# Causal attention by head on one core: q and k by one projection, their copies laid out by DMA, and a new order of calls

## The chip, the cores and the metric

The kernel runs on one core of a Trainium2 chip. The metric is the device time of one execution in microseconds (us); lower is better. TensorE is PE in the profile, VectorE is DVE, ScalarE is ACT, GpSimd is POOL, and SyncE, which only issues DMAs here, is SP. PE's weight loads are listed apart, as PEld.

## What is computed

The program is an attention layer with a small graph network, three layer norms with residuals, and then two layers of local attention with a feed-forward block. The change touches only the first part. Per batch (2) and head (16), with 1024 tokens and heads of 64 features, the reference computes:

```python
xn = layer_norm(x, gamma_in)
q = (xn @ Wq).reshape(b, n, HEADS, DHEAD).transpose(0, 2, 1, 3) * scale      # scale = 1/8
k = (xn @ Wk).reshape(b, n, HEADS, DHEAD).transpose(0, 2, 1, 3)
v = (xn @ Wv).reshape(b, n, HEADS, DHEAD).transpose(0, 2, 1, 3)
sim = jnp.where(causal_mask, mask_value, jnp.einsum('bhid,bhjd->bhij', q, k))
attn = jax.nn.softmax(sim, axis=-1)
out = jnp.einsum('bhij,bhjd->bhid', attn, v)
adj = jnp.clip(attn + eye, 0.0, 1.0)          # by head
for l in range(2):
    h = adj @ (feats @ gnn_w[l] + gnn_b[l]) / deg
    feats = gelu(h + feats)
out = out + feats @ lin_w + lin_b
return layer_norm(out @ Wo, gamma_out)
```

## The kernel before

**Heads.** The 32 pairs of batch and head are numbered t = 0 to 31 (NH = 32). Each engine runs a program of its own, written out by hand as a list of calls; its instructions run in that order, and semaphores (`p_...` raised by PE, `a_...` by ACT, `d_...` by DVE, `w_...` by POOL) say when an operand is ready. One pass of the loop over t is called a head below. It holds the scores and the product with the values of head t, the row maxima (`smax`) of head t + 1, the projection (`proj`) of head t + 2, the second graph layer (`graph2`, `graph2b`) of head t - 1 and of head t, and the output product (`tailT`, `tail`) of head t - 2.

**Two parts for each number.** Matmuls read operands rounded to fp32r, so every operand is kept as a rounded part (hi) and a remainder (lo). A product of two such numbers is the sum of hi·hi, hi·lo and lo·hi.

**q and k.** `WD` holds the weights of a head twice side by side, so that the projection on PE (L520 to L538) gives the same 64 features in partitions 0 to 63 and 64 to 127 of a bank. There are four of them for each head: k and q, and two column halves c of 512 tokens; each is three matmuls. ACT (`proj`, L1024 to L1032) writes the hi part of all 128 partitions into `K1` or `Q1`. DVE (`lower`) writes the lo part: that of q (L1509) over partitions 64 to 127 of `Q1`, that of k (L1507) into partitions 0 to 63 of `K2`. POOL (`upper`, L1340) copies the hi part of q into `Q2`. A tile of scores (L618, L619) is then K1·Q1, which is k_hi·(q_hi + q_lo), plus K2·Q2, which is k_lo·q_hi; `K2` has two rows of ones under it and `Q2` the negated row maximum as hi and lo, so that the maximum comes off in the same matmul.

**The row maximum.** `smax` on PE (L581) makes score tiles with queries in the partitions, DVE takes their maxima (L1532), and after the last of 12 tiles combines them and splits them in hi and lo in `NM` (L1537, L1539, L1541). `mrow` turns them into rows: eight matmuls with an identity (L598, four for each half c), then two copies of 2x512 on ACT (L1051) into `Q2`.

**Tiles.** The causal triangle of 1024x1024 is cut into 12 tiles of 128 keys by 512, 384, 256 or 128 queries. For each tile there are two matmuls of scores, ACT's two exponentials (L1061 and L1062, into `Es` and `Eh`), DVE's remainder `El` (L1554), three matmuls of `av` (L636 to L638) and two of `graph2` (L671, L672). Score tiles alternate between banks 2 and 3, so that `scores(t, k)` waits for the exponential of tile k - 2; `smax` tiles alternate between banks 0 and 1. `graph2` ends each half with four matmuls (L676) into bank 5, which ACT copies out (`hopend`, L1095) before `graph2(t, 4)` may write there.

**DMA.** Between the loads at the start and the end of the first part, SP issues nothing at all. The second part of the program copies values between partitions by DMA (L453 and L455: 64 partitions x 2 KB, 128 KB each).

## Time and profile before

| | us |
|---|---|
| median of 3 runs (1625.11 to 1625.67) | 1625.44 |
| the profiled execution | 1620.1 |
| its span on the core, first to last instruction | 1618.3 |
| from the start to the first tile of scores | 39.3 |
| heads 1 to 29, from 81.64 to 1056.46 | 974.8 |
| the second part, from about 1131 to the end | about 487 |

The granted clock was 0.972 on average. Of the span PE was busy for 1469.1 us (91%), DVE for 1285.7 (79%), ACT for 1054.1 (65%), POOL for 419.2 (26%). In the rows, "x12" is a count, and the time after "busy" or before the engine's name is that of the group. In a timeline a row is start, duration, engine, line, operation, output<-input and shape; matmuls overlap, so the start of one to the start of the next tells how far it moves PE on, not its duration.

### The profile page before, as it was taken

Reading aid. Unit: us, or ns where it says so; the run is one execution under the profiler, and the core shown is the slowest. Engines: PE = TensorE matmul, PEld = TensorE weight load, DVE = VectorE, ACT = ScalarE, POOL = GpSimd, SP = SyncE. Lnnn points to the kernel's source line nnn. Section 1 sums busy time; section 2 is a strip of 40 time slices with the busy share of each in tenths; the row PEclk is TensorE's granted clock in tenths of the full one; section 3 lists DMA queues with packets and bytes.
Section 4 is the critical chain, followed back from the end, with each engine's and each line's share of the span. In section 5 each row is a group of like instructions: output and inputs, shape, how many; then the busy total and the mean of one; then the engine's idle time right before and its main releaser. Section 6 shows DMA issues by size and latency. Waiting matters only on the chain.

```text
span 1618.3 us, 30002 instructions
## 1 busy us (share of the span) xinstructions
PE 1469.1 (91%) x10578; PEld 1157.4 (72%) x10578; DVE 1285.7 (79%) x3374; ACT 1054.1 (65%) x2403; POOL 419.2 (26%) x544
## 2 busy tenths in 40 slices
PE   5999999999999999999999999998467899999996
PEld 4678877788788887788877888777245566666664
DVE  6588887888888788888888888875577888878875
ACT  3577676666676767767667676764245777787673
POOL 2122223222332222322233222211322342223221
PEclk9899999999999999999999999999778999999999
DMA  4000000000000000000000000000400010000100
GB/s 122 1 1 2 1 1 1 1 1 1 1 1 1 1 1 1 1 1 1 1 1 1 2 1 1 1 1 1 111 14 20 17 26 19 21 21 17 28 18 20
DMA packets 23199, 19.67 MB, mean 12 GB/s; under 512 B 8414, under 2 KB 18314, under 8 KB 23050
## 3 DMA queue, kind: packets, MB, share of 16 engines
q1 hardware_dynamic: 23050, 17.76, 4.3%
q8 instruction: 84, 1.38, 0.4%
q14 instruction: 65, 0.53, 0.1%
HBM read 8.84 MB, written 1.05 MB: 6 GB/s over the span
## 4 chain that ended last, share of the span: by engine, by line
issue 33%; PE 27%; DVE 20%; ACT 10%; POOL 8%; DMA 0%; SPq 0%; POOLq 0%; DVEq 0%; ACTq 0%
ACT t L1213 5%; PE PS L671 3%; DVE t L1554 2%; PE PS L672 2%; PE PS L706 2%; POOL t L1307 2%; DVE t L1585 2%; POOL t L1350 2%; PE PS L618 2%; PE PS L581 2%; POOL t L1340 2%; PE PS L619 1%; DVE t L1756 1%; DVE t L1782 1%; DVE t L1740 1%
## 5 line engine op out<-in xcount | busy, mean ns | idle before, releaser
L1061 ACT ACTIVATE t<-PS 128x512 f32<-128x512 f32 (+3 forms) x384 | 191.3, 498 | 222.3 <-PE PS L621 136.5
L1554 DVE TENSOR_TENSOR t<-t 128x512 fp32r<-128x512 f32 (+3 forms) x384 | 246.6, 642 | 48.8 <-ACT t L1062 47.3
L1532 DVE TENSOR_REDUCE t<-PS 128x1 f32<-128x512 f32 (+3 forms) x384 | 208.0, 549 | 24.2 <-PE PS L581 24.0
L1062 ACT ACTIVATE t<-PS 128x512 fp32r<-128x512 f32 (+3 forms) x384 | 191.7, 499 | 0.0
L1350 POOL TENSOR_TENSOR t<-t 128x256 f32<-128x256 f32 x64 | 39.2, 613 | 551.7 <-DVE t L1574 551.7
L671 PE MATMUL PS<-t 128*128 128x512 f32 (+3 forms) x384 | 141.8, 369 | 21.6 <-ACT t L1095 21.6
L1213 ACT ACTIVATE t<-PS,t 128x128 f32<-128x128 f32 x256 | 113.2, 464 | 67.4 <-DVE t L1786 67.3
L1415 POOL TENSOR_TENSOR t<-t 128x16 f32<-128x16 f32 x32 | 92.8, 2900 | 239.7 <-DVE t L1742 239.7
L636 PE MATMUL PS<-t 128*66 128x512 f32 (+3 forms) x384 | 137.3, 358 | 16.2 <-DVE t L1554 16.2
L581 PE MATMUL PS<-t 128*128 128x512 f32 (+3 forms) x384 | 141.0, 378 | 3.6 <-DVE t L1532 2.7
L618 PE MATMUL PS<-t 128*128 128x512 f32 (+3 forms) x384 | 143.6, 374 | 0.1
L619 PE MATMUL PS<-t 66*128 66x512 f32 (+3 forms) x384 | 134.5, 350 | 0.0
L638 PE MATMUL PS<-t 128*66 128x512 f32 (+3 forms) x384 | 129.6, 338 | 0.0
L637 PE MATMUL PS<-t 128*66 128x512 f32 (+3 forms) x384 | 129.1, 336 | 0.0
L672 PE MATMUL PS<-t 128*128 128x512 f32 (+3 forms) x384 | 129.0, 348 | 0.0
L1307 POOL TENSOR_TENSOR t<-t 128x2 f32<-128x2 f32 (+1 forms) x42 | 33.8, 804 | 272.4 <-DVE t L1462 180.7
L671 PEld LDWEIGHTS PS<-t 128*128 128x128 f32 x384 | 73.4, 191 | 37.4 <-ACT t L1095 26.1
L1551 DVE SCALAR_TENSOR_TENSOR t<-t 128x128 f32<-128x128 f32 x256 | 72.6, 284 | 29.0 <-ACT t L1061 29.0
L618 PEld LDWEIGHTS PS<-t 128*128 128x128 f32 x384 | 74.4, 194 | 17.0 <-issue 2.5
L581 PEld LDWEIGHTS PS<-t 128*128 128x128 f32 x384 | 75.1, 196 | 13.0 <-DVE t L1532 4.7
L1032 ACT ACTIVATE t<-PS 128x512 fp32r<-128x512 f32 x128 | 76.3, 596 | 12.1 <-PE PS L538 8.3
L672 PEld LDWEIGHTS PS<-t 128*128 128x128 f32 x384 | 73.7, 192 | 9.8
(191 smaller groups left out, 4152.6 us busy)
## 6 DMA issues: line engine op xcount, KB each, us to landing
t<-t SPq DMA_DIRECT2D x60, 128.0 KB, 2.3
t<-in_L_ffn_wqkv SPq DMA_DIRECT2D x2, 768.0 KB, 6.9
t<-in_L_attn_Wv SPq DMA_DIRECT2D x2, 512.0 KB, 7.9
t<-in_c_rot SPq DMA_DIRECT2D x2, 512.0 KB, 4.7
out<-t SPq DMA_DIRECT2D x4, 256.0 KB, 2.3
t<-in_L_ffn_w SPq DMA_DIRECT2D x2, 341.0 KB
t<-in_L_attn_x SPq DMA_DIRECT2D x2, 256.0 KB, 3.2
t<-in_L_attn_Wq SPq DMA_DIRECT2D x1, 512.0 KB, 5.5
```

What stands on the lines that cost most here:

```text
L581: m = e.matmul(bank(b)[:, 0:hi - lo], Q1[r][:, ib * P:(ib + 1) * P], K1[r][:, lo:hi], start=True, stop=not diag)
L618: e.matmul(b[:, 0:n], K1[r][:, jb * P:(jb + 1) * P], Q1[r][:, i0:i0 + n], start=True, stop=False)
L619: m = e.matmul(b[:, 0:n], K2[r][:, jb * P:(jb + 1) * P], Q2[r][:, i0:i0 + n], start=False, stop=not diag)
L636: e.matmul(dst, VH[r][:, jb, :], Eh[:, o:o + n], start=(jb == 0), stop=False)
L638: m = e.matmul(dst, VH[r][:, jb, :], El[:, o:o + n], start=False, stop=(jb == 4 * c + 3))
L671: e.matmul(dst, F2[:, jb, :], Eh[:, o:o + n], start=(jb == 0), stop=False)
L672: e.matmul(dst, F2[:, jb, :], El[:, o:o + n], start=False, stop=False).then_inc(p_hop.up((t, k)), 1)
L1061: e.activation(Es[:, k % NS, 0:n], b[:, 0:n], ACT.Exp).then_inc(a_es.up((t, k)), 1)
L1062: e.activation(Eh[:, o:o + n], b[:, 0:n], ACT.Exp).then_inc(a_eh.up((t, k)), 1)
L1213: m = e.activation(E[u][:, n, :], bank(SB + j)[:, c * P:(c + 1) * P], ACT.Exp, bias=nmx[u][:, n:n + 1], scale=sc8[w][:, n:n + 1], accum_ou ...
L1532: e.tensor_reduce(n[:, c, ib:ib + 1], bank(k % 2)[:, 0:hi - lo], AX.X, ALU.max, negate=True).then_inc(d_max.up((t, k)), 1)
L1554: e.tensor_tensor(El[:, o:o + n], Es[:, k % NS, 0:n], f32(Eh[:, o:o + n]), ALU.subtract).then_inc(d_el.up((t, k)), 1)
```

## The change

All of it is in the first part of the program. The two heads' weights Wk and Wq stand side by side in `WD`, which is half as large, and one projection gives k in partitions 0 to 63 and q in 64 to 127. ACT writes both hi parts into `K1`, with a scale by partition from the new tile `qsc` (1 and 0.125), and DVE both lo parts into `Q1`. SP then moves what the scores need elsewhere: `part` copies q_hi to `Q2` and k_lo to `K2` (four transfers of 64 partitions x 2 KB), `double` copies k_hi to the other half of `K1` and q_hi back into `Q1` (two of 64 x 4 KB). `smax` and `scores` wait for `double`. POOL's `upper` is gone, and `widen` does half as much.

The maximum is no longer split: one matmul in full f32 turns the eight columns into eight rows, ACT copies 8x128 into the new tile `MR`, and SP's `mrow` moves it (4 KB) into one row of `Q2`. `K2` and `Q2` have 65 rows.

The order of calls changes on all engines. The projection of head t + 2 on PE stays near the end of head t; `smax(t + 1, 0)`, which opened the head, now stands behind the third tile of scores.

```diff
+            def part(t):
+                r = t % RB
+                for c in range(2):
+                    sl = slice(c * 512, (c + 1) * 512)
+                    q.wait_ge(*a_hi[t, c])
+                    e.dma_start(f32(Q2[r][0:64, sl]), f32(K1[r][64:128, sl])).then_inc(s_apart[c], 16)
+                    q.wait_ge(*d_low[t, c])
+                    e.dma_start(f32(K2[r][0:64, sl]), f32(Q1[r][0:64, sl])).then_inc(s_apart[c], 16)
+            def double(t):
+                r = t % RB
+                q.wait_ge(*apart(t, 0))
+                q.wait_ge(*apart(t, 1))
+                e.dma_start(f32(K1[r][64:128, :]), f32(K1[r][0:64, :])).then_inc(s_twice, 16)
+                e.dma_start(f32(Q1[r][0:64, :]), f32(Q2[r][0:64, :])).then_inc(s_twice, 16)
+            def mrow(t):
+                q.wait_ge(*a_row[t])
+                e.dma_start(f32(Q2[t % RB][64:65, :]).rearrange("a (k p) -> a k p", k=8), f32(MR[:])).then_inc(s_row, 16)
+            part(0)
+            double(0)
+            for t in range(NH):
+                if t + 1 < NH:
+                    part(t + 1)
+                mrow(t)
+                if t + 1 < NH:
+                    double(t + 1)
...
-                e.matmul(bank(b), WD[t % RB][:, 0, i, :], xh[:, x0_:x1_], start=True, stop=False)
-                e.matmul(bank(b), WD[t % RB][:, 1, i, :], xh[:, x0_:x1_], start=False, stop=False)
-                e.matmul(bank(b), WD[t % RB][:, 0, i, :], xl[:, x0_:x1_], start=False,
-                         stop=True).then_inc(p_proj.up((t, which, c)), 1)
+                e.matmul(bank(b), W[:, 0, :], xh[:, x0_:x1_], start=True, stop=False)
+                e.matmul(bank(b), W[:, 1, :], xh[:, x0_:x1_], start=False, stop=False)
+                e.matmul(bank(b), W[:, 0, :], xl[:, x0_:x1_], start=False, stop=True).then_inc(p_proj.up((t, c)), 1)
...
-                q.wait_ge(*d_low[t, "q", 1])
-                q.wait_ge(*a_hi[t, "k", 1])
+                q.wait_ge(*twice(t))
...
-                for k in range(4):
-                    m = e.matmul(bank(4)[0:66, k * P:(k + 1) * P], NM[:, 4 * c + k, :], identR[:], start=True, stop=True)
+                e.matmul(bank(4)[0:8, 0:P], nm[t % 2][:, 0, :], identF[:], start=True, stop=True).then_inc(p_row.up(t), 1)
...
-                q.wait_ge(*a_row[t, 1])
-                q.wait_ge(*w_q2[t, 1])
-                q.wait_ge(*d_low[t, "q", 1])
-                q.wait_ge(*d_low[t, "k", 1])
+                q.wait_ge(*row_ready(t))
+                q.wait_ge(*twice(t))
...
-                e.activation(T1[:, c * 512:(c + 1) * 512], bank(b), ACT.Copy, scale=sc).then_inc(a_hi.up((t, which, c)), 1)
+                e.activation(K1[t % RB][:, c * 512:(c + 1) * 512], bank(b), ACT.Copy, scale=qsc[:, 0:1]).then_inc(a_hi.up((t, c)), 1)
...
-                if which == "k":
-                    m = e.tensor_tensor(K2[r][0:64, sl], bank(b)[0:64, :], f32(K1[r][0:64, sl]), ALU.subtract)
-                else:
-                    m = e.scalar_tensor_tensor(Q1[r][64:128, sl], bank(b)[64:128, :], 0.125, f32(Q1[r][64:128, sl]),
-                                               ALU.mult, ALU.subtract)
+                e.scalar_tensor_tensor(Q1[r][:, sl], bank(b), qsc[:, 0:1], f32(K1[r][:, sl]), ALU.mult,
+                                       ALU.subtract).then_inc(d_low.up((t, c)), 1)
...
-                smax(t + 1, 0)
                 scores(t, 0)
...
+                scores(t, 2)
+                smax(t + 1, 0)
```

On PE, at the end of a head, the rows of before are these: L536 to L538 are a projection, L598 is `mrow`, L657 `graph1`, L671 and L672 `graph2`, L618 the next head's first scores behind L581, its first `smax`.

```order
L536 MATMUL PS<-t 128x512
L537 MATMUL PS<-t 128x512
L538 MATMUL PS<-t 128x512
L598 MATMUL PS<-t 66x128 x4
L657 MATMUL PS<-t 128x130 x4
L536 MATMUL PS<-t 128x512
L537 MATMUL PS<-t 128x512
L538 MATMUL PS<-t 128x512
L671 MATMUL PS<-t 128x512
L672 MATMUL PS<-t 128x512
L671 MATMUL PS<-t 128x256
L672 MATMUL PS<-t 128x256
```

The changed kernel has there, with `graph2` at L694, L695 and L699, `graph1` at L680, `mrow` at L624 and the scores of the next head at L641:

```order
L694 MATMUL PS<-t 128x512
L695 MATMUL PS<-t 128x512
L680 MATMUL PS<-t 128x130 x4
L694 MATMUL PS<-t 128x256
L695 MATMUL PS<-t 128x256
L624 MATMUL PS<-t 8x128
L694 MATMUL PS<-t 128x384
L695 MATMUL PS<-t 128x384
L694 MATMUL PS<-t 128x128
L695 MATMUL PS<-t 128x128
L699 MATMUL PS<-t 128x128 x4
L694 MATMUL PS<-t 128x512
```

No projection is left in the last stretch, and `mrow` is a single matmul, behind which five tiles of `graph2` still stand before the scores that need its result.

On DVE, at the same place, before has two remainders of q (L1509) and two of k (L1507), and three small operations for the maximum behind the last two reductions (L1532):

```order
L1532 TENSOR_REDUCE t<-PS 128x1 x2
L1537 TENSOR_TENSOR t<-t 128x4
L1539 CAST t<-t 128x8
L1541 TENSOR_TENSOR t<-t 128x8
L1600 TENSOR_TENSOR t<-t 128x4x64
L1509 SCALAR_TENSOR_TENSOR t<-PS,t 64x512 x2
L1608 TENSOR_TENSOR t<-t 128x4x64
L1507 TENSOR_TENSOR t<-PS,t 64x512
```

The changed kernel has the remainders (L1498) first, and the reductions (L1520) behind them:

```order
L1583 TENSOR_TENSOR t<-t 128x4x64
L1498 SCALAR_TENSOR_TENSOR t<-PS,t 128x512 x2
L1520 TENSOR_REDUCE t<-PS 128x1
L1591 TENSOR_TENSOR t<-t 128x4x64
L1520 TENSOR_REDUCE t<-PS 128x1
L1524 TENSOR_TENSOR t<-t 128x4
```

Two remainders instead of four stand there, one small operation instead of three, and the maximum is ready only after the remainders.

SP has nothing in this stretch before. The changed kernel has seven transfers for each head, `part` (L435, L437), `mrow` (L448) and `double` (L443, L444):

```order
L435 DMA t<-t 64x512
L437 DMA t<-t 64x512
L435 DMA t<-t 64x512
L437 DMA t<-t 64x512
L448 DMA t<-t 1x8x128
L443 DMA t<-t 64x1024
L444 DMA t<-t 64x1024
```

`double` of head t + 2 is issued behind `mrow` of head t + 1, and so not before that maximum is out of ACT.

## Rows read from the trace of the kernel before

**Rows 1.** Windows: length, busy us (count) PE, PEld, DVE, ACT, POOL, clock, DMA.
```profile
451.85:485.27 33.42, 32.36 (x221) 26.98 (x220) 27.42 (x74) 23.19 (x50) 8.69 (x15) 1.00 0.01 1
81.64:1056.46 974.82, 937.46 (x6365) 781.12 (x6364) 819.22 (x2267) 673.52 (x1422) 261.23 (x418) 1.00 0.00 1
```
**Rows 2.** Waits of PE from 81.64 to 1056.46: total us, times, longest us.
```profile
PE PS L671 <- ACT t L1095: 19.6, 29, 0.7
PE PS L636 <- DVE t L1554: 14.2, 29, 0.8
```
**Rows 3.** Timeline of PE in head 12: start us, duration us.
```profile
456.74 1.95 PE L706 MATMUL PS<-t 128*128 128x128 f32 x16
458.44 0.47 PE L618 MATMUL PS<-t 128*128 128x512 f32 x1
...
474.89 0.40 PE L536 MATMUL PS<-t 128*128 128x512 f32 x1
...
475.59 0.39 PE L636 MATMUL PS<-t 128*66 128x512 f32 x1
...
478.86 0.40 PE L598 MATMUL PS<-t 128*66 128x128 f32 x4
479.10 1.11 PE L657 MATMUL PS<-t 66*128 66x130 f32 x8
```
**Rows 4.** Groups of DVE by line: busy us, mean ns, idle before.
```profile
L1507 DVE TENSOR_TENSOR t<-PS,t 64x512 fp32r<-64x512 f32 x64 | 43.3, 677 | 1.0
L1509 DVE SCALAR_TENSOR_TENSOR t<-PS,t 64x512 fp32r<-64x512 f32 x64 | 41.9, 692 | 7.5 <-ACT t L1032 6.5
...
L1480 DVE SCALAR_TENSOR_TENSOR t<-PS,t 128x512 fp32r<-128x512 f32 x4 | 3.0, 748 | 1.2 <-ACT t L1010 1.2
```
**Rows 5.** Groups of ACT by line.
```profile
L1032 ACT ACTIVATE t<-PS 128x512 fp32r<-128x512 f32 x128 | 76.3, 596 | 12.1 <-PE PS L538 8.3
...
L1051 ACT CAST t<-PS 2x512 fp32r<-2x512 f32 x64 | 37.0, 578 | 13.6 <-PE PS L598 12.8
...
L1010 ACT ACTIVATE t<-PS,t 128x512 fp32r<-128x512 f32 x4 | 2.8, 689 | 0.9 <-PE PS L484 0.9
```
**Rows 6.** DMA issues of the page: count, KB each, median us to landing.
```profile
t<-t SPq DMA_DIRECT2D x60, 128.0 KB, 2.3
```
**Rows 7.** The same transfers' line: time of one issue in ns, min/median/max.
```profile
L455 SPq DMA_DIRECT2D t<-t x28: 461/590/1210, 1157.9 to 1552.3; - x28
```
**Rows 8.** A window of the second part (last: DMA share, GB/s).
```profile
1300.00:1360.00 60.00, 56.37 (x509) 38.62 (x509) 50.25 (x100) 45.11 (x124) 20.15 (x10) 1.00 0.09 21
```
**Rows 9.** Timeline of ACT at the end of head 12.
```profile
482.90 0.58 ACT L1095 COPY t<-PS 128x512 f32<-128x512 f32 x1 [0.44 <-PE PS L676]
```
**Rows 10.** Timeline of ACT at the start of head 12.
```profile
452.60 0.60 ACT L1061 ACTIVATE t<-PS 128x512 f32<-128x512 f32 x1 [0.44 <-PE PS L621]
453.09 0.59 ACT L1062 ACTIVATE t<-PS 128x512 fp32r<-128x512 f32 x1
```
**Rows 11.** Timeline of PE in head 30: waits before two groups.
```profile
1081.80 0.28 PE L636 MATMUL PS<-t 128*66 128x128 f32 x1 [1.05 <-DVE t L1554]
...
1082.96 0.45 PE L598 MATMUL PS<-t 128*66 128x128 f32 x4 [0.76 <-DVE t L1541]
```
**Rows 12.** A window of head 30 (columns as in Rows 1).
```profile
1085.00:1086.00 1.00, 1.00 (x8) 0.98 (x7) 0.68 (x2) 0.00 (x0) 0.25 (x1) 0.50 0.00 0
```
**Rows 13.** Timeline of DVE in head 12: a difference of two SBUF tiles.
```profile
475.74 1.39 DVE L1554 TENSOR_TENSOR t<-t 128x128 fp32r<-128x128 f32 x1
```
**Rows 14.** Timeline of POOL at the same time.
```profile
475.69 1.28 POOL L1371 TENSOR_TENSOR t<-t 128x512 f32<-128x512 f32 x1 [1.75 <-DVE t L1615]
```
**Rows 15.** Timeline of PE: the first tiles of smax.
```profile
22.74 0.62 PE L581 MATMUL PS<-t 128*128 128x512 f32 x2 [0.81 <-DVE t L1509]
```
**Rows 16.** Windows at the start (columns as in Rows 1).
```profile
24.00:28.00 4.00, 3.88 (x27) 3.12 (x27) 2.65 (x7) 1.29 (x4) 0.00 (x0) 1.00 0.27 83
...
36.00:40.00 4.00, 2.71 (x11) 1.77 (x11) 1.06 (x4) 1.15 (x2) 0.00 (x0) 0.54 0.00 0
```

More of the change, by code:

```diff
@@ L352, in program @@
         s_vs = [sem(f"vs{i}") for i in range(4)]
+        s_apart = [sem(f"s_apart{c}") for c in range(2)]
+        s_twice = sem("s_twice")
+        s_row = sem("s_row")
         ld = {n: sem("l_" + n) for n in ("xa", "xb", "xc", "id", "wq", "wk", "gin", "wv", "w0", "wv2", "cm", "wg", "ww1",
@@ L729, in tensor @@
                     turn(t - 4, 6)
+                graph2(t - 1, 9)
                 scores(t, 1)
+                graph2(t - 1, 6)
+                scores(t, 2)
+                smax(t + 1, 0)
                 smax(t + 1, 1)
+                scores(t, 3)
                 tailT(t - 2, 0)
@@ L738, in tensor @@
                     linear(1, 6)
-                tailT(t - 2, 1)
-                graph2(t - 1, 6)
-                scores(t, 2)
-                scores(t, 3)
+                scores(t, 4)
+                tail(t - 2, 0)
                 smax(t + 1, 3)
@@ L1045, in projv, with mrow @@
                 e.copy(VH[r][:, ks, 0:DH], pv[:, :, 0:DH]).then_inc(a_v.up((t, c)), 1)
[L1047 removed]
+            def mrow(t):
                 if t >= NH:
                     return
[L1050 to L1051 removed]
+                q.wait_ge(*p_row[t])
+                if t:
+                    q.wait_ge(*row_ready(t - 1))
+                e.copy(MR[:], bank(4)[0:8, 0:P]).then_inc(a_row.up(t), 1)
             def scores(t, k):
@@ L1685, in vector @@
                     began(1)
+                smax(t + 1, 0)
                 scores(t, 1)
@@ L1698, in vector @@
                 smax(t + 1, 4)
-                scores(t, 5)
+                share(t - 1, 1)
                 smax(t + 1, 5)
```

282 lines of the change are left out of this document (113 added, 169 removed).

## The prediction

> **What bounds the kernel now.** I read the busy time by windows first. A steady head takes 33.42 us and PE is busy for 32.36 of them; DVE with 27.42 and ACT with 23.19 have room [rows 1]. Over heads 1 to 29 it is 937.46 of 974.82 us. The waits of PE come next: only two kinds matter, 19.6 us before the tile of graph2 that needs bank 5 emptied by ACT, and 14.2 us before the small tile of av that needs DVE's remainder, 0.7 and 0.5 us for each head [rows 2]. So the first part is bound by PE almost throughout, and work taken from PE should come off the time, unless the operands now come too late. The second part (some 487 us) is not touched.
>
> **PE, removed.** In the timeline one projection starts at 474.89 and the next group at 475.59, so three matmuls move PE on by 0.70 us [rows 3]. Two of four projections go: 1.40 us. Since a group costs up to 0.05 more where the weights ahead of it aren't hidden, I take 1.45. The eight small matmuls of mrow move PE on by 0.24 us for each four (478.86 to 479.10), 0.48 in all. The one f32 matmul that replaces them isn't in this trace with 8 output rows; the nearest row is the f32 product of 128x128, 16 matmuls (two for each product) in 458.44 - 456.74 = 1.70 us, so 0.21 us [rows 3]. Its bounds are 0.06, if it were as cheap as one of the old, and 0.21; I take the latter, as the same type and length. Net: 1.45 + 0.48 - 0.21 = **1.7 us for each head**.
>
> **The other engines.** DVE loses four remainders of 0.68 us and gains two of about 0.75, the row with a scale by partition [rows 4]: 2.74 - 1.50 = 1.24 us, and two small operations more. ACT loses four copies of 0.60 and two of 0.58, and gains two of 0.69 and one small one, bounded by 0.58 [rows 5]: at least 1.6 us less. POOL loses two copies. None of these engines sets the pace at 31 to 32 us a head (27.42 - 1.24 is 26.2), so this gain is priced at nothing; what it buys is slack for the waits below.
>
> **The waits PE has.** The gap of 0.68 us before graph2(t, 4) remains: the last product into bank 5 must be copied by ACT, a copy of 0.58 us behind 0.44 us of idle time [rows 9], and nothing in the new order stands between the two on PE. The gap before av(t, 11) should go, because a projection less and graph2b stand ahead, and DVE has more time: -0.5 us. New ones may come. At the head's start, the third scores tile (which needs the exponential of the first) stands after only two tiles of scores and two of graph2, some 1.5 us of columns; ACT starts 0.75 us after PE's start at 451.85 and has both exponentials out at 453.68, 1.83 us [rows 1, 10]. That is a wait of about 0.3 us. And DVE, whose order waits for smax tile 6 before it does the remainder of scores tile 5, is late for smax tile 11 by 0 to 0.45 us if I follow its list with the durations of the trace; I take 0.2. Sum: old gaps down by 0.5, new ones up by 0.5. **No change.**
>
> **The row of the maximum.** Behind mrow on PE stand five tiles of graph2: 8 matmuls of 512 or 384 columns, two of 128 and four small ones, 2.3 us at 0.23 for each 512 columns, plus the gap. With mrow's own 0.2 and, counted from start to start, 0.85 for the gap, the next scores start 3.5 us after mrow. The chain it must hide: matmul 0.2, its result 0.2 later, ACT's copy 0.3 (up to 0.58, [rows 5]), and the transfer. The nearest row is 128 KB in 2.3 us from issue to landing [rows 6]; 4 KB can hardly take longer. Sum 3.0 to 3.3 us. It fits by 0.2 to 0.5 us, as long as ACT is free, which it is: gelu2 ahead of it must wait for POOL, which by my count is done some 2 us before mrow's result. I price it at nothing. If the cover is gone, each 0.1 us costs 3 us in all.
>
> **part and double.** One issue takes SP 0.46 to 0.59 us [rows 7]. The projection of head t + 2 ends 3.9 us before mrow; ACT and DVE need 0.69 and 0.75 for the last half [rows 4, 5]. Both remainders are ready some 2 us after the last projection, and the last of the four small transfers lands 2.3 us later, at about the time of mrow's copy on ACT. double is issued behind mrow's transfer, 1.3 us after mrow began on PE. Its length isn't in the trace. The transfers of the second part move 21 GB/s at a share of 0.09 [rows 8], 233 GB/s when all 16 engines work, so 128 KB take 0.56 us and 256 KB 1.12. One such transfer would land after 2.3 + 0.56 = 2.9 us and the second, queued behind it, 1.1 us later: 4.0 us, so 5.3 us after mrow. PE wants it at smax(t + 2, 0), behind the 3.5 us above and 1.9 us of scores and graph2: 5.4 us. Bounds: 2.3 us (as if bytes cost nothing) is far inside, and half the rate would be 6.2 us, a wait of 2.1 us for each head. I take the row's rate and a price of nothing, but this is the thinnest cover in the change.
>
> **A rule about these transfers.** In rows, 128 KB take 2.3 us [rows 6]. The Trainium skill, "DMA: Bandwidth & Descriptors", section "Anatomy of one DMA", gives about 2.0 us for any transfer plus its bytes at 436 GB/s. By that page double would be an estimate of 2.0 + 1.2 = 3.2 us for both; no row here shows that rate.
>
> **POOL against DVE.** A difference of two SBUF tiles on DVE that should take 0.28 us took 1.39 beside an operation of POOL of 1.28 [rows 13, 14]. In the new order POOL's long addition for graph2b comes behind feats(t, 0) and meets DVE's feats(t, 0): DVE is held up by some 0.4 us there, ahead of the remainders. The maximum still comes before PE asks for it. Priced at nothing.
>
> **Start and end.** The first smax tile was at 22.74 [rows 15]. Now it needs remainders, four small transfers and double. The queues are busy with loads until about 26 us (share 0.27 between 24 and 28, [rows 16]), so double lands at 29 to 31, 6 to 8 us later. But the second projection and both of v are then done, and what follows is bound by twelve maxima on DVE instead of those and the remainders of head 1, four of 0.68 us [rows 4]. Then 2.5 us for the row's transfer. Net 2 us later, -2 to +6. The clock was at 0.54 from 36 to 40 already [rows 16]. Head 30 has no projection: it gains 0.2.
>
> **The sum.** 29 steady heads x 1.7 = 49 us, head 0 about 2, the start costs 2: 49 us. On the profile's own 1620.1 that is 1571; the median is 5 us above that execution, so **1576 us**.
>
> **Rivals.** (a) *The cover of a transfer is too thin.* Landing times here are a median of a part of the program where few are in flight; here seven follow each other. A wait of 0.5 to 1.5 us for each head on smax(t + 2, 0) or on scores(t + 1, 0) gives 15 to 45 us back: 1591 to 1621. For it: my margins are 0.1 and 0.2 to 0.5 us. Against: the sums take the longer of the values. (b) *The order on DVE becomes the wait.* Every smax tile waits for the maximum two before. If DVE's idle wait for tile 6 pushes the rest back by 0.5 us more than I counted, it is 1590. Against: 26.2 us of work in 31.7. (c) *Slower than before.* If double takes 6 us or more, PE waits 2 us or more in each head. In head 30 PE waited 1.05 and 0.76 us shortly after one another, and then had a granted clock of 0.50, the 1.2 GHz level, for over 3 us [rows 11, 12], which costs half of that time. The threshold is thus near 1.8 us: beyond it each head loses the wait and 1.7 us more, 3.5 in place of the 1.7 won, and the kernel takes 1625 + 29 x 1.8 = 1678. The Trainium skill has this as a rule: "TensorE: Matmul & The Clock Gate", section "HAM oscillation", tells of a kernel that waits for a DMA in every step and starts every step at the low clock. By that rule, the trace of head 30 agrees; the 29 steady gaps of 0.7 us are followed by no such fall. (d) *More than the matmuls.* ACT and DVE run less late, and the remaining gap shrinks too: up to 0.5 us for each head, 1562.
>
> **Chances.** Forecast with its own bounds, 1562 to 1590: 0.62. (a) 0.20. (b) 0.06. (c) 0.05. (d) 0.07. The range leaves out the upper half of (a), (c), and the outer part of (d): 1563 to 1606. About 0.2% (3 us) is what a measurement of this kernel can tell from no change. Only (c) is slower; a wait that eats exactly the gain is the only way to no change: faster 0.93, same 0.02, slower 0.05.
>
> **What would show it.** PE busy in a steady head at 30.6 to 30.7 us and the head at 31.5 to 32.0. Waits of PE: L694 (graph2) on ACT 0.7; small ones on the third scores tile and on smax; none on a DMA at scores or smax. double landing 3 to 4 us after its issue. What makes it wrong: DMA as a releaser of PE with over 0.3 us a head, or a granted clock under 1.00 in the steady heads.

## The result, and the profile after

The changed kernel takes **1607.2 us** (median; 1605.8 to 1609.0), the kernel before 1625.4 beside it on the same chip: a ratio of 0.989, with a 95% interval of 0.987 to 0.991. The forecast was 1576 us with a range of 1563 to 1606. So the sign was right, the gain is 18 us instead of 49, and the time lies just outside the range. The profiled execution took 1606.2 us, and its span is 1604.5.

First the windows that answer to [rows 1]: head 12, heads 1 to 29, the start up to the first scores tile, and head 0.

```profile
core 0: us, PE busy (x) PEld busy (x) DVE busy (x) ACT busy (x) POOL busy (x), PEclk, DMA share, GB/s
451.37:483.80 32.43, 31.49 (x209) 25.46 (x209) 24.17 (x70) 21.37 (x47) 6.98 (x13) 1.00 0.16 34
...
92.10:1043.70 951.60, 913.44 (x6017) 736.81 (x6016) 727.75 (x2151) 619.66 (x1335) 216.34 (x357) 1.00 0.16 33
0.00:47.19 47.19, 21.69 (x91) 16.10 (x91) 20.67 (x65) 9.29 (x16) 8.34 (x29) 0.81 0.54 138
47.19:92.10 44.91, 42.54 (x196) 28.48 (x197) 23.29 (x70) 20.41 (x45) 3.81 (x8) 0.79 0.14 29
```

A steady head went from 33.42 to 32.43 us, and PE's busy time in it from 32.36 to 31.49, where 30.65 was forecast. DVE and ACT fell as counted. The span's balance is this, with the boundaries of before at 39.26 and 81.64 us. The first scores tile comes 7.9 us later (forecast: 2). Head 0 takes 44.9 us where it took 42.4, 2.5 more (forecast: 2 less). Heads 1 to 29 take 951.6 in place of 974.8, 23.2 less (forecast: 49). The rest is 1.0 shorter. Together that is 13.8 us of span.

The waits of PE that answer to [rows 2], in heads 1 to 30 (total us, times, longest us):

```profile
PE PS L694 <- ACT t L1111: 20.2, 30, 0.7
PE PS L613 <- DVE t L1520: 8.6, 15, 0.8
PE PS L613 <- DMA t<-t: 3.9, 7, 0.8
PE PS L680 <- ACT t L1085: 2.7, 17, 0.2
```

The wait of graph2 for ACT stayed, as forecast. The 14.2 us before av(t, 11) are gone. Three small kinds are new: smax tile 11 for DVE, the first smax tile for a transfer in seven heads (2, 5, 8, 11, 17, 20, 23), and graph1(t, 1) for ACT's copy.

The end of head 12 on PE, which answers to [rows 3] (start us, duration us):

```profile
475.21 0.48 PE L572 MATMUL PS<-t 128*128 128x512 f32 x1
475.53 0.39 PE L573 MATMUL PS<-t 128*128 128x512 f32 x1
475.76 0.40 PE L574 MATMUL PS<-t 128*128 128x512 f32 x1
...
480.08 0.39 PE L624 MATMUL PS<-t 128*8 128x128 f32 x2
480.39 0.44 PE L694 MATMUL PS<-t 128*128 128x384 f32 x1
```

Two things can be read from the start times. The f32 mrow moves PE on by 0.31 us (480.08 to 480.39), not 0.21. And two equal matmuls can differ: the first of the projection, behind the small ones of graph2b, moves PE on by 0.32 us (475.21 to 475.53), the second by 0.23 (475.53 to 475.76). The 0.09 us are a weight load that shows because what stands ahead of it is short. PE's weight loads at the same place say so:

```profile
475.19 0.19 PEld L572 LDWEIGHTS PS<-t 128*128 128x128 f32 x1
475.30 0.19 PEld L573 LDWEIGHTS PS<-t 128*128 128x128 f32 x1
475.53 0.19 PEld L574 LDWEIGHTS PS<-t 128*128 128x128 f32 x1
```

The weights of the first matmul begin to load at 475.19, 0.02 us ahead of their own matmul; those of the second begin 0.23 us ahead of theirs (475.30 and 475.53). I call such a place an **exposed load**. No view counts it as a wait: it is "busy" time of PE.

So I went through the starts of PE in one head and split each step from start to start: the columns at 2.4 GHz (0.21 us for 512; 0.11 for 128 columns of plain f32), the waits the profile records, and what is left. Where more than 0.045 us is left and no wait is recorded, it is an exposed load. These places leave 0.05 to 0.13 us each. In head 12 of the changed kernel and of the kernel before, the weight load of such a matmul begins 0.04 us ahead of it (median), and that of the other long matmuls 0.23 us. Other choices for the limits move the column by up to 0.2 us and two places. Two kernels of the next section stand in the table too: the new order alone with the old data path, and the new data path alone with the old order. All are heads at a clock of 1.00.

| one steady head, us | columns | exposed loads (places) | recorded waits | other | head |
|---|---|---|---|---|---|
| before | 29.11 | 2.14 (28) | 1.06 | 1.13 | 33.43 |
| new order alone | 29.11 | 2.81 (33) | 1.59 | 1.23 | 34.74 |
| new data path alone | 27.56 | 2.27 (27) | 3.91 | 1.40 | 35.14 |
| the change | 27.56 | 3.00 (34) | 0.94 | 0.93 | 32.43 |

The columns fell by 1.55 us. Then 0.86 us came back in the column of exposed loads, with six more places and some dearer ones, and "other" fell by 0.20. The net of 0.66 us is the larger part of what is missing in PE's busy time (31.49 and not 30.65).

"Other" holds, beside small remainders, the step into each recorded wait, which is 0.16 to 0.18 us longer than columns and wait together and counts as busy. In head 12, four matmuls of L699 start at 481.02 and the next group at 482.30: of these 1.28 us, 0.45 are columns and 0.67 the recorded wait. The kernel before has two recorded waits (of 0.1 us or more) in this head, the change three, the new order alone four, the new data path alone three.

The transfers, which answer to [rows 6]: the page, and the lines of `double` by themselves (L443, then L444). Those of `part` still land after 2.3 us (median).

```profile
t<-t SPq DMA_DIRECT2D x64, 256.0 KB, 3.4
```
```profile
L443 SPq DMA_DIRECT2D t<-t x32: 462/479/526, 29.9 to 1041.5; - x32
...
DMA to landing us min/median/max: 2.9/2.9/3.1
```
```profile
L444 SPq DMA_DIRECT2D t<-t x32: 580/597/597, 30.4 to 1042.0; - x32
...
DMA to landing us min/median/max: 3.6/3.7/4.9
```

The estimate of 2.9 us for the first transfer of `double` was met. The second, from its own issue 0.5 us later, takes 3.7, and up to 4.9 in some heads.

### The profile page after: what moved, and what is told of

It is laid out like the page before. It is cut to its first block, busy times and chain, and to the rows that moved or that the text cites. A ratio compares the mean times of both kernels' runs of the same rounds, so it can differ in the third digit from the quotient of the medians.

```text
span 1604.5 us, 29173 instructions
## 1 busy us (share of the span) xinstructions
PE 1444.8 (90%) x10194; PEld 1109.6 (69%) x10194; DVE 1187.4 (74%) x3247; ACT 995.6 (62%) x2307; POOL 370.2 (23%) x480
## 4 chain that ended last, share of the span: by engine, by line
PE 43%; DVE 25%; issue 13%; ACT 11%; DMA 3%; POOL 3%; SPq 1%; DVEq 0%; POOLq 0%; ACTq 0%
ACT t L1222 5%; DVE t L1520 4%; PE PS L613 4%; PE PS L729 3%; PE PS L708 3%; PE PS L694 3%; DVE t L1537 3%; PE PS L641 3%; DMA t<-t 3%; PE PS L642 2%; PE PS L695 2%; PE PS L661 2%; PE PS L659 2%; PE PS L660 2%; PE PS L680 2%
## 5 line engine op out<-in xcount | busy, mean ns | idle before, releaser
L1520 DVE TENSOR_REDUCE t<-PS 128x1 f32<-128x512 f32 (+3 forms) x384 | 211.3, 551 | 81.4 <-PE PS L615 56.8
L1537 DVE TENSOR_TENSOR t<-t 128x512 fp32r<-128x512 f32 (+3 forms) x384 | 212.3, 553 | 10.9 <-ACT t L1078 10.8
L694 PE MATMUL PS<-t 128*128 128x512 f32 (+3 forms) x384 | 150.2, 391 | 22.1 <-ACT t L1111 21.6
L613 PE MATMUL PS<-t 128*128 128x512 f32 (+3 forms) x384 | 141.4, 392 | 24.5 <-DMA t<-t 12.5
L641 PE MATMUL PS<-t 128*128 128x512 f32 (+3 forms) x384 | 149.8, 390 | 2.7 <-DMA t<-t 2.2
L642 PE MATMUL PS<-t 65*128 65x512 f32 (+3 forms) x384 | 134.4, 350 | 0.0
L695 PE MATMUL PS<-t 128*128 128x512 f32 (+3 forms) x384 | 129.2, 345 | 0.0
L613 PEld LDWEIGHTS PS<-t 128*128 128x128 f32 x384 | 73.4, 198 | 41.8 <-DVE t L1520 20.2
L694 PEld LDWEIGHTS PS<-t 128*128 128x128 f32 x384 | 73.3, 191 | 38.2 <-ACT t L1111 26.1
L641 PEld LDWEIGHTS PS<-t 128*128 128x128 f32 x384 | 75.0, 195 | 20.5 <-ACT t L1078 9.9
L680 PEld LDWEIGHTS PS<-t 66*128 66x128 f32 x512 | 64.6, 190 | 24.2 <-ACT t L1085 18.3
L1111 ACT COPY t<-PS 128x512 f32<-128x512 f32 x64 | 37.4, 585 | 67.6 <-PE PS L699 67.6
```

The costliest lines, as they stand in the source:

```text
L613: m = e.matmul(bank(b)[:, 0:hi - lo], Q1[r][:, ib * P:(ib + 1) * P], K1[r][:, lo:hi], start=True, stop=not diag)
L641: e.matmul(b[:, 0:n], K1[r][:, jb * P:(jb + 1) * P], Q1[r][:, i0:i0 + n], start=True, stop=False)
L642: m = e.matmul(b[:, 0:n], K2[r][:, jb * P:(jb + 1) * P], Q2[r][:, i0:i0 + n], start=False, stop=not diag)
L694: e.matmul(dst, F2[:, jb, :], Eh[:, o:o + n], start=(jb == 0), stop=False)
L695: e.matmul(dst, F2[:, jb, :], El[:, o:o + n], start=False, stop=False).then_inc(p_hop.up((t, k)), 1)
L1520: e.tensor_reduce(n[:, c, ib:ib + 1], bank(k % 2)[:, 0:hi - lo], AX.X, ALU.max, negate=True).then_inc(d_max.up((t, k)), 1)
```

## The experiments

Twelve kernels were run, in three groups, each beside the kernel before on the same chip (medians 1623.7, 1622.0 and 1622.6 us). Where this text says "less" or "later" with no other name, it compares with the changed kernel, from which all start but one (the first of the pair below) and the two that start from the combined kernel. The kernel before itself differs by up to 3.4 us between these chips, so a difference of a few us in the time alone shows little; such readings rest on the windows.

The start adds to this. In the profiled executions of four kernels whose start is the same as the changed kernel's (projection twice, graph1 later, DVE's order, no mask) head 0 took 48.9 to 50.1 us at a granted clock of 0.71 or 0.72, and not 44.9 at 0.79.

### Is PE still what sets the pace?

```diff
+                if t > 1:
+                    e.matmul(bank(b), W[:, 0, :], xh[:, x0_:x1_], start=True, stop=False)
+                    e.matmul(bank(b), W[:, 1, :], xh[:, x0_:x1_], start=False, stop=False)
+                    e.matmul(bank(b), W[:, 0, :], xl[:, x0_:x1_], start=False, stop=True)
                 e.matmul(bank(b), W[:, 0, :], xh[:, x0_:x1_], start=True, stop=False)
```

> Each of the two projections of a head from head 2 on is issued twice, so that TensorE gets six more matmuls a head and nothing else changes. If TensorE's own work sets the length of a head (31.5 us busy of 32.4), the copies cost their whole time, about 1.4 us a head, 41 us in all: about 1648 us. If waits set it, the copies fill them and the time stays between 1607 and 1620 us.

Measured: 1647.5 us (1645.5 to 1649.8), 40 us more. A steady head:

```profile
470.10:503.92 33.82, 32.88 (x216) 26.59 (x215) 23.83 (x70) 21.37 (x47) 7.07 (x13) 1.00 0.15 32
```

Six matmuls more cost 1.39 us of busy time and 1.39 us of the head. PE sets the pace, and the price of a projection, 0.7 us each, was right. What the change takes away is thus not lost to another engine.

### The order alone, and the data path alone

The first kernel is the one before with the change's order of calls on all engines; its two projections more stand together behind graph2(t, 2), directly ahead of mrow, and its second mrow behind graph2(t, 1). The end of a head in its list on PE (its lines 789 to 797):

```python
                av(t, 11)
                graph2(t, 0)
                graph1(t, 1)
                graph2(t, 2)
                proj(t + 2, "k", 0, 0)
                proj(t + 2, "k", 1, 1)
                mrow(t + 1, 0)
                graph2(t, 1)
                mrow(t + 1, 1)
```

> The kernel before with the new order of calls alone: four projections, eight matmuls for the maximum, POOL's copies and no transfers; the k projections stand behind graph1(t, 1) on PE, the start is that of before. Theory order: of the 0.7 us a head that the change wins less than forecast, 0.5 are weight loads that the new order leaves exposed (a short matmul ahead of a full weight load costs 0.1; 30 such places in a head before, 37 after) and the rest two new waits, less the one that goes. The order alone should then cost 0.2 to 0.5 us a head: 1631 to 1640. Rival: the order is as good or better by itself (it removes the wait of 0.5 before av 11) and the loss comes from the new data path: 1610 to 1625.

Measured: 1685.0 us (ratio 1.037, 1.033 to 1.040), far more than both theories had. Its head 12, and its waits from 92 to 1100 us:

```profile
480.26:515.00 34.74, 33.15 (x222) 26.86 (x221) 26.28 (x74) 23.23 (x50) 8.53 (x15) 1.00 0.00 1
```
```profile
PE PS L671 <- ACT t L1094: 18.9, 28, 0.7
PE PS L598 <- ACT t L1050: 18.0, 28, 0.7
PE PS L581 <- DVE t L1530: 8.3, 15, 0.8
PE PS L657 <- ACT t L1068: 4.6, 28, 0.2
```

PE does exactly the work of the kernel before and is busy 33.15 us instead of 32.36, 0.79 more. In the table the exposed loads grow by 0.67 us, 33 places for 28. That is the plainest evidence for the missing term: **the new order costs PE's time in each head where no wait is to be seen**. How much is less plain, since the steps into two more recorded waits account for some 0.3 of the 0.79 us; 0.4 to 0.5 are left.

Of the waits, L598 for ACT is of my own making: the second mrow waits until ACT has copied the first. Those 0.65 us stand 2 us ahead of the gap of 0.67. In 11 of heads 1 to 29 the granted clock fell to 0.50, the 1.2 GHz level, for some 3 us, each time within 1 us of the second of these waits, although the two are the same in all 29 heads. One such fall lies between 443 and 447 us:

```profile
444.00:479.00 35.00, 33.43 (x217) 26.97 (x217) 25.35 (x73) 22.23 (x48) 7.39 (x13) 0.96 0.00 1
443.50:446.50 3.00, 3.00 (x10) 2.19 (x9) 0.39 (x2) 1.78 (x3) 2.66 (x7) 0.50 0.00 0
```

This kernel's time is therefore no price of the order, nor is the length of its undisturbed heads, which hold the wait of my own making.

The second kernel is the changed one with the order of calls of before: the second projection of head t + 2 stands directly ahead of mrow, and smax(t + 2, 0) opens the next head. Between mrow and that smax tile stand graph1 and seven tiles of graph2, so mrow is not directly ahead of it, as the expectation has it.

> The changed kernel's data path (one projection of k and q, one mrow, operands laid out by the transfers of 128 and 256 KB), but the order of calls of the kernel before. There mrow stands directly ahead of the smax tiles and little work hides the two transfers of 256 KB, which landed 4.0 us or more after they were issued. If the new order is what hides them, smax waits 2 us or more for DMA in each head and the clock falls in some: 1690 to 1720 us. If the transfers are hidden anyway, the time is about that of the changed kernel, 1600 to 1615 us.

Measured: 1722.2 us (ratio 1.062, 1.058 to 1.065). Waits from 92 to 1100 us, and a head without and one with a fall of the clock:

```profile
PE PS L613 <- DMA t<-t: 81.6, 28, 3.5
```
```profile
576.69:611.83 35.14, 31.23 (x209) 25.26 (x208) 25.97 (x70) 21.23 (x46) 6.97 (x12) 1.00 0.15 31
429.67:468.01 38.34, 33.79 (x210) 27.17 (x209) 26.23 (x70) 21.51 (x46) 6.97 (x12) 0.93 0.14 29
```

PE waits 2.8 to 3.5 us for `double` in each head. What makes it late is `part`: in head 14 the second projection starts at 602.25, the last transfer of `part` lands at 607.21, and only at 607.27 and 607.79 is `double` issued, 4.1 us behind mrow (603.17) where the changed kernel has 1.5. So neither part helps alone: the path needs the order to hide its transfers, and the order by itself only costs. Together they win 1.0 us a head.

This pair gives the order's price on PE a second time. At the same matmuls and with three recorded waits in each, PE is busy for 31.23 us in the old order and for 31.49 in the new. The exposed loads differ by 0.73 us, but "other" by 0.47 the other way. Net, by the two pairs, the order costs PE 0.3 to 0.5 us a head, 8 to 13 us in 29 heads, and not the 0.7 that the column of exposed loads shows by itself.

### How thin is the cover of the transfer?

```diff
             for t in range(NH + 2):
+                smax(t + 1, 0)
                 scores(t, 0)
...
                 scores(t, 2)
-                smax(t + 1, 0)
                 smax(t + 1, 1)
```

> The changed kernel, but the first smax tile of a head stands ahead of the first scores tile on PE and DVE, where it stood before the change. Measures the cover of double: it landed just in time for its place behind the third scores tile, 1.9 us of PE's work later. Theory cover: PE waits about 1.8 us more in each head at this tile, and part of that is won back behind it: a head takes 33.5 to 34.5, the kernel 1640 to 1670. If such a wait makes the granted clock fall in each head (as two waits of 1.05 and 0.76 us did in head 30 of the kernel before), another 1.7 us a head: 1690 to 1720. Rival: double is early and the place costs nothing: 1605 to 1610.

Measured: 1696.0 us (ratio 1.044, 1.041 to 1.047), the dearer case: 13 of the heads 2 to 29 have a mean clock of 0.95. The wait is 1.9 us a head:

```profile
PE PS L613 <- DMA t<-t: 56.1, 29, 2.9
```

Moving the first smax tile ahead by three tiles of scores and two of graph2, 2.26 us of PE's time in the changed kernel (451.37 to 453.63), opens a wait of 1.9 us. Hence the cover in the changed kernel is about 0.3 us. Its trace says the same: L444 is issued at 482.10 and lands after 3.64 us, at 485.74, and the smax tile that needs it starts at 486.08; where PE does wait, the tile starts 0.04 us after the landing. Counted from mrow's start at 480.08, the transfers took 5.7 us (forecast 5.3) and had 6.0 (forecast 5.4). The chain that ended at smax(t + 1, 0) of head 17 in the changed kernel shows what is in it and what happens when the transfer takes longer (start us, us, what):

```profile
609.87 0.33 PE PS L624 x2
...
610.22 0.26 ACT t L1067
...
610.50 0.69 SPq L448
...
611.29 0.48 SPq L443
...
611.82 4.93 DMA t<-t
616.75 0.04 issue
616.80 0.61 PE PS L613 x2
```

Of these 6.9 us the transfer alone is 4.9 where it is 3.6 in the head before, and PE waits 0.81 us. What goes with such a late landing is a third of the page's queues:

```profile
q8 instruction: 81, 1.33, 0.3%
```

Its packets have 16 KB, and in each of the seven heads in which PE waits for the transfer one of them starts while the transfer is under way. In the traces of the twelve kernels that have this transfer it is the same: of 62 second transfers of `double` with such a packet (the first of each kernel left out) 52 took 4.4 to 5.0 us and the rest 3.6 to 4.0, and of 310 without one none took over 4.1. No run took these packets away, so this is a coincidence in many traces, and the cause is not shown. To see whether a little more cover is enough, a kernel with more work ahead of smax was run (it contains other edits too; its base is the combined kernel further down):

```diff
                 scores(t, 2)
+                graph2(t - 1, 8)
                 smax(t + 1, 0)
```

> As the combined kernel, with TensorE's graph2(t-1,8) moved ahead of smax(t+1,0), which puts about 0.5 us more work over the second 256 KB transfer. If the waits of 0.3 to 0.8 us in every third head are a transfer that lands late against thin cover, they shrink to 0.3 us or less and the time falls by 2 to 5 us below the combined kernel. If they follow from what comes before smax on TensorE and not from the transfer, they stay and the time too.

Measured: 1590.4 us, 1.5 more than its base, within the error. In the trace the first half of the expectation came true: from 85 to 1050 us the waits for DMA fell from 4.8 us (8 times) to 0.5 us (twice). But what PE no longer waits for there it waits for on DVE, in heads with extra work of DVE:

```profile
PE PS L613 <- DVE t L1525: 17.6, 16, 1.3
```

The base has 10.0 us in this row. The tile of graph2 had stood later, ahead of scores(t, 6), where it gave DVE time.

### The two new waits on PE

```diff
                 graph2(t, 0)
-                graph1(t, 1)
                 graph2(t, 2)
+                graph1(t, 1)
                 mrow(t + 1)
```

> TensorE's order graph2(t,0), graph1(t,1), graph2(t,2) becomes graph2(t,0), graph2(t,2), graph1(t,1), next to mrow. If the changed kernel lost 0.3 us a head to the wait of graph1(t,1) for ScalarE's copy of av and to one more change between types, a head becomes 0.3 to 0.4 us shorter, 8 to 12 us in all: 1595 to 1599 us. If something later is late instead, mrow is later too and the time stays at 1605 to 1609 us.

Measured: 1600.8 us (1593.7 to 1605.1; ratio 0.987, 0.983 to 0.990, not apart from the changed kernel's). Its profiled execution took 1605.1 us and has the long head 0 (49.3 us at 0.71). Head 12 takes 32.29 us, 0.14 less, which is the wait of 0.15 that is gone. Nothing was gained on exposed loads: mrow behind graph1, both f32, shows one just as well.

```diff
-                smax(t + 1, 6)
                 scores(t, 5)
-                smax(t + 1, 7)
                 projv(t + 1, 0)
+                smax(t + 1, 6)
+                smax(t + 1, 7)
```

> VectorE does scores(t,5) and the projection's sums of the next head ahead of its work on the sixth and seventh smax tiles of the next head. If the last smax tile waits because VectorE frees its PSUM buffer late (gap 0.12 us in most heads, 0.3 to 0.8 in others, 8.6 us in fifteen heads together), that wait goes and the time falls by 5 to 10 us, to 1597 to 1602 us. If what VectorE now does later is late in its turn, the time stays at 1605 to 1610 us.

That is VectorE's list. Measured: 1605.4 us (ratio 0.990, 0.988 to 0.992, not apart either). Head 12 is 0.3 us shorter, and its wait is gone, as the first theory says. Heads 18 to 25 are not:

```profile
453.18:485.30 32.12, 31.30 (x209) 25.38 (x208) 24.07 (x70) 21.27 (x47) 6.95 (x13) 1.00 0.16 34
680.16:713.37 33.21, 31.49 (x209) 25.49 (x208) 26.15 (x78) 21.28 (x47) 7.97 (x13) 1.00 0.15 32
```

In them DVE has 2 us more to do, from the second part's preparation, and PE waits 0.85 us for an earlier maximum instead of 0.8 for that of tile 11. Each theory held in one kind of head.

### What a short matmul costs

```diff
+                diag = diag and t < 2
                 m = e.matmul(bank(b)[:, 0:hi - lo], Q1[r][:, ib * P:(ib + 1) * P], K1[r][:, lo:hi], start=True, stop=not diag)
```

> The changed kernel without the eight short causal mask matmuls (128 columns, bf16) of smax in heads from head 2 on, so that the row maxima are taken over unmasked scores too. Their own slots are 8 times 0.04 us a head, 0.3 us, 10 us in all: 1597 us. If behind each of them a later weight load also shows by about 0.08 us, a head loses 0.8 to 1.0 us of work, 24 to 29 us in all: 1578 to 1583 us, or less of it where a wait for VectorE or for the transfer takes its place (1583 to 1592 us).

Measured: 1591.9 us (ratio 0.982, 0.978 to 0.985), between the two, with a fall of the clock in heads 20 and 21. Head 13 takes 31.85 us where it took 32.39: of the 0.54 us, 0.32 are the masks' own time, and 0.27 are exposed loads that went (2.93 to 2.67 us, 33 places to 31; waits and the rest changed by 0.05). So a mask costs 0.07 us rather than 0.04, and not 0.12. It exposes a load at some of its places and not at others; "behind each of them" was too simple.

### The start

```diff
-            e.dma_start(wqkv0, I["L0_ffn_wqkv"][0]).then_inc(ld["wqkv0"], 16)
-            e.dma_start(gam_out[:], I["L0_attn_gamma_out"].rearrange("(a d) -> a d", a=1).broadcast_to([P, DM])).then_inc(ld["gout"], 16)
-            e.dma_start(x0[:, 8:16, :], x_tiles[:, 8:16, :]).then_inc(ld["xc"], 16)
...
             part(0)
             double(0)
+            e.dma_start(wqkv0, I["L0_ffn_wqkv"][0]).then_inc(ld["wqkv0"], 16)
+            e.dma_start(gam_out[:], I["L0_attn_gamma_out"].rearrange("(a d) -> a d", a=1).broadcast_to([P, DM])).then_inc(ld["gout"], 16)
+            e.dma_start(x0[:, 8:16, :], x_tiles[:, 8:16, :]).then_inc(ld["xc"], 16)
```

> The changed kernel, but the loads of the second half of x, of wqkv0 and of gamma_out (1.3 MB) are issued behind the first part and double instead of ahead of them. Theory queue: the first smax tile waits 8.6 us for these transfers because they stand behind the loads (one landed only after 8.2 us, against 2.3 later on). Without the loads ahead of them the wait shrinks to two landings and the issues, about 6 us after the copies, so the first smax tile comes 3 to 5 us earlier and the whole is 1602 to 1605 us. Rival, latency alone: the transfers are serial anyway and the tile comes less than 1 us earlier: 1606 to 1608.

Measured: 1603.8 us (ratio 0.988, 0.986 to 0.991), not apart from the changed kernel's; the start is read from the trace. Each transfer of the first `part` lands after 2.3 to 2.4 us. The wait for the first operands falls from 8.6 to 3.2 us, and the first scores tile comes at 40.0, 7.2 us sooner. Head 0 then takes 3.1 us more and has more of the low clock, which ends between 66 and 67 us in both; but the four kernels with the unchanged start have 4.0 to 5.2 us more, so this run doesn't show that the earlier start is what made it longer. First the changed kernel's two waits, then this kernel's two windows:

```profile
PE PS L613 <- DMA t<-t: 8.6, 1, 8.6
PE PS L641 <- DMA t<-t: 2.2, 1, 2.2
```
```profile
0.00:40.03 40.03, 19.96 (x90) 14.32 (x90) 20.66 (x65) 9.29 (x16) 8.34 (x29) 0.82 0.64 162
40.03:88.09 48.06, 45.71 (x196) 31.29 (x196) 23.36 (x70) 20.51 (x45) 3.76 (x8) 0.73 0.13 27
```

The other cause by itself, PE kept busy in both waits, with 78 and 24 transposes whose results nobody reads:

```diff
+            q.wait_ge(*d_turn[0])
+            for _ in range(78):
+                e.transpose(bank(0)[:, 0:P], identF[:], identF[:])
             for k in range(NTL):
                 smax(0, k)
             mrow(0)
+            for _ in range(24):
+                e.transpose(bank(0)[:, 0:P], identF[:], identF[:])
```

> The changed kernel with 78 idle transposes on PE ahead of the first smax tile and 24 behind the first mrow, so that PE has work in the two waits for a transfer at the start; nothing else moves. Theory clock: of the 10.4 us that start and head 0 lost together, some 2 to 5 are the granted clock of 0.50 in the smax tiles and in head 0, which follows the idle 8.6 us. With the clock kept up the first scores tile comes 1 to 2 us earlier and head 0 takes 38 to 41 instead of 44.9 us: 1599 to 1603 in all. Rival: the low clock comes anyway, from the sparse smax tiles (as before the change), or it costs nothing because DVE sets the pace: 1606 to 1608.

Measured: 1599.4 us (ratio 0.986, 0.983 to 0.988). Head 0 falls from 44.9 to 37.1 us at a clock of 1.00; the first scores tile stays where it was, though 1 to 2 us less had been expected:

```profile
47.50:84.60 37.10, 34.09 (x199) 24.23 (x198) 23.09 (x70) 20.31 (x45) 3.79 (x8) 1.00 0.11 24
```

### All four together, and one step too far

The combined kernel has the four edits, with 30 transposes in place of 78, since less is to be waited for.

> The changed kernel with the loads behind the first operand transfers, 30 idle transposes ahead of the first smax tile and 24 ahead of the first scores tile, graph2(t,2) ahead of graph1(t,1), and VectorE's scores(t,5) and projection sums ahead of its sixth and seventh smax tile. If the start's two causes (queued loads, a clock at 0.50) act apart and add up, the first scores tile begins at 38 to 40 us and head 0 takes 37 to 38 us, 14 to 16 us less than the changed kernel up to the end of head 0; the two edits of the order take another 0.3 to 0.45 us from each ordinary head (about 8 us in all): 1582 to 1588 us. If they get in each other's way, 1592 us or more.

Measured: **1588.9 us** (1587.1 to 1591.9), a ratio of 0.979 (0.976 to 0.981) to the kernel before. It is clear of both kernels, and none here is faster. Three windows:

```profile
467.34:499.24 31.90, 31.23 (x209) 25.52 (x208) 24.01 (x71) 21.31 (x47) 6.93 (x13) 1.00 0.16 34
0.00:41.84 41.84, 26.61 (x144) 21.57 (x145) 20.48 (x65) 9.31 (x16) 8.37 (x29) 0.88 0.66 168
41.84:80.17 38.33, 35.57 (x197) 25.55 (x196) 23.39 (x70) 20.30 (x45) 3.52 (x7) 0.95 0.10 21
```

This head, an ordinary one, is 0.5 us shorter, more than the 0.45 expected at most; heads 1 to 29 together are 6.1 us shorter (945.5 and not 951.6), where about 8 was expected. Up to the end of head 0 it is 11.9 us instead of 14 to 16: the first scores tile comes at 41.8 and not at 38 to 40. Why those 2 us are missing stays open; in the kernel with more cover, whose start is the same code, that tile came at 45.0 us, so the start varies by as much from one execution to another.

The last kernel joined tail(t - 2, 0) and tail(t - 2, 1), and put DVE's extra work behind its seventh smax tile:

```diff
                 scores(t, 4)
-                tail(t - 2, 0)
...
                 scores(t, 5)
+                tail(t - 2, 0)
                 tail(t - 2, 1)
```

> As the kernel with more cover, with tail(t-2,0) moved next to tail(t-2,1) on TensorE and VectorE, and VectorE's extra work of some heads (normed, onward) moved behind its seventh smax tile. If weight loads show where plain f32 groups stand apart, joining the two saves about 0.08 us in each head on TensorE (2 to 3 us in all), and heads 18 to 25 lose their wait of 0.8 us for VectorE: 5 to 8 us below the kernel with more cover. If the loads are hidden and VectorE is late by its total work, the time stays within 2 us.

Measured: 1634.9 us (ratio 1.008, 1.005 to 1.010). Both hopes fell. An ordinary head is 0.24 us longer, not 0.08 shorter, though one exposed load went; and in the heads with extra work it now delays DVE's remainders, so that two waits follow each other and the clock falls:

```profile
477.60:509.76 32.16, 31.47 (x209) 25.46 (x208) 23.99 (x71) 21.30 (x47) 6.91 (x13) 1.00 0.16 34
673.85:711.98 38.13, 35.12 (x210) 28.08 (x209) 25.99 (x79) 21.52 (x47) 8.05 (x13) 0.91 0.13 29
```

## Why the prediction was off, step by step

- **PE, removed: right but for 0.1.** Projection and mrow together moved PE on by 1.60 us less, where 1.7 was forecast. The projection gave 1.44, and the f32 mrow costs 0.31 and not 0.21: the nearest row was inside a group of 16, where the load of the next weights is hidden, and a lone one is not.
- **The step that failed** is the sum that takes for PE's gain the matmuls removed and nothing else: what the new order and the new waits do to PE's busy time was put at nothing. The text had the fact in hand ("a group costs up to 0.05 more where the weights ahead of it aren't hidden") and used it for the projection only. The exposed loads grew by 0.86 us a head, 25 us in 29 heads; net of "other" it is 0.66 us, 19 us. The two pairs at equal work show 0.3 to 0.5 us of it as the order's; how the rest divides between the data path and the steps into waits is not shown.
- **The waits: the net of nothing was right.** Recorded waits went from 1.06 to 0.94 us in head 12, and from 37.4 to 38.2 us in heads 1 to 29. av(t, 11) gave 0.4 to 0.5 back; smax 11 takes 0.1 in ordinary heads, and 0.8 in heads 18 to 25. The forecast 0.3 us before the third scores tile did not come; 0.15 before graph1(t, 1) did, which it had not.
- **The row of the maximum: right in what it says.** scores(t + 1, 0) never waits for it in steady heads. But its terms (2.3, 0.2 and 0.85 us) add up to 3.35 and not to 3.5, and with 3.35 the cover of `double` would have been 5.25 us, less than the 5.3 needed. Measured were 3.7 us from mrow to the scores and 2.3 from there to smax, where 1.9 was taken. That the cover held is in part luck.
- **part and double: sized nearly right, spread missed.** 5.7 us against 6.0 was true in 22 of heads 1 to 29. In the other seven the transfer took 0.8 to 1.3 us longer, and PE waited for 3.9 us in all. The second transfer landed 4.2 us after the first was issued, against 4.0 by the rate of the second part and 3.2 by the fit in the Trainium skill's "DMA: Bandwidth & Descriptors", section "Anatomy of one DMA", which is one for transfers that GpSimd issues.
- **DVE's order: right in kind.** 0 to 0.45 us were computed for smax 11; 0.12 came in most heads, and 0.8 in those with extra work of DVE, which the forecast had not looked at.
- **The start: wrong by 10 us.** 2 us later and 2 us less in head 0 were forecast; 7.9 later and 2.5 more came. The forecast saw `double` land at 29 to 31 us, and it landed after 34, because a `part` transfer queued behind the loads took up to 8.2 us (L437; 6.2 for L435); with the loads later the four of the first `part` took 2.3 to 2.4. What was not followed at all is the clock: PE stood still for 8.6 us, and the granted clock was at 0.50, the 1.2 GHz level, beyond 62 us:

```profile
24.00:28.00 4.00, 1.77 (x16) 1.63 (x15) 2.17 (x5) 1.30 (x4) 1.69 (x6) 1.00 0.92 194
28.00:32.00 4.00, 0.00 (x0) 0.00 (x0) 0.00 (x0) 0.00 (x0) 0.00 (x0) 0.62 0.33 75
32.00:36.00 4.00, 1.17 (x4) 0.68 (x4) 0.78 (x2) 0.00 (x0) 0.00 (x0) 0.50 0.88 203
...
47.19:62.00 14.81, 14.52 (x32) 6.88 (x32) 5.38 (x19) 5.20 (x12) 0.00 (x0) 0.50 0.17 35
```

- **The rivals.** (a), a cover too thin, was the nearest in its time (1591 to 1621) but not in its cause: the transfer costs 4 us and not 15 to 45. (c) did not happen here, and its mechanism is real: in the kernels with smax first and with the old order a transfer's wait of 1.9 to 2.8 us brought falls of the clock, and 1696 and 1722 us where it gave 1678. The condition was close by: 2.3 us of PE's work ahead of the tile. Its threshold of 1.8 us did not hold, neither way: falls followed waits of 0.65 and 0.67 us in 11 of 29 heads, and one of 2.8 us was followed by none in some heads with the old order. The rule of the Trainium skill that went with it, "TensorE: Matmul & The Clock Gate", section "HAM oscillation", agrees with these heads in part: with the old order, after nearly the same wait of 2.8 us, one head ran at 1.00 throughout (35.14 us) and another at a mean of 0.93 (38.34).
- **The range** missed by 1 us because its cases shared one sum. The exposed loads, which were in none, would have taken 19 us net from all of them.

In sum, 49.3 us were forecast for heads 1 to 29 and nothing for the rest. Counted as in the table over these 29 heads, 4.8 are missing in the columns, 25.9 went to exposed loads and 0.8 to waits (late transfers and DVE's maxima, against the wait of av(t, 11) that went), and 5.3 came back in "other": 23.1 us. Start and head 0 lost 10, and the end won 1. That gives 14 us of span.

## What to carry to other kernels

Price a new order of calls even where it adds no work and no wait: count, in the list of the engine that sets the pace, the places where a long weight load stands behind a short matmul or at the edge of a plain f32 group, before and after. An engine's "busy" time is not its work; take start-to-start times, and compare them with the columns. When a transfer moves onto the path, look at its longest landing and not only its median, and where a kernel's start gets a new wait, look at what the clock does to the work behind it. And when two kernels are compared by their columns of PE, count their recorded waits too: here each brought 0.16 to 0.18 us that counts as busy.

## What the runs showed of the chip

- A weight load behind a short matmul shows as 0.05 to 0.13 us of PE's busy time (0.32 in place of 0.23 for the same matmul), 27 to 34 times in the heads of the table. Which places show it, I can describe but not foretell: taking eight short masks away removed only two (four, if the limit is set otherwise).
- The step into a recorded wait of PE is 0.16 to 0.18 us longer than the columns and the wait, and counts as busy.
- Two transfers of 256 KB issued 0.5 us apart land after 2.9 and 3.7 us, the second up to 4.9, and in twelve traces over 4.1 us only where a packet of the instruction queue q8 fell into it; one of 128 KB alone after 2.2 to 2.3, and up to 8.2 among loads.
- Two waits of only 0.65 and 0.67 us, 2 us apart, were followed by a granted clock of 0.50 in 11 of heads 1 to 29 of the kernel with the order alone. The one of 0.67 with no such wait near ahead of it never was, in heads 2 to 29 of the kernel before and of the changed one. The Trainium skill's "TensorE: Matmul & The Clock Gate" has a section, "HAM oscillation", on waits that repeat in each step; these are shorter than the waits for DMA that it tells of.
- 78 and 24 transposes for nothing, over two waits at the start, gave 8 us back in head 0.
